# Two mixture-of-experts stages in one long kernel: the token dispatch is split around a turn, and two shared chunks move into the last expert

## The chip, the cores and the metric

The kernel runs on 1 core of one Trainium2 chip. The metric is the device time of one execution in microseconds (us), the median of several runs. The engines are named as in the profile: PE is TensorE's matmul, PEld its weight load, DVE is VectorE, ACT is ScalarE, POOL is GpSimd, SP is SyncE, whose queue issues the weight loads.

## What is computed

The reference is one forward pass over a residual stream `x` of 256 tokens of width 768, with eight layers that alternate graph layers and feed-forward layers:

```
x = x + L0_gnn(layernorm(x));  x = x + L0_ffn(layernorm(x))
x = x + L1_gnn(layernorm(x));  x = x + L1_ffn(layernorm(x))
x = x + L2_gnn(layernorm(x));  x = x + L2_ffn(layernorm(x))
x = x + L3_gnn(layernorm(x));  x = x + L3_ffn(layernorm(x))
```

The change touches two of the eight. Both route each token to its two best of 8 experts and add an expert that all tokens share:

```
L0_ffn: gates = top2(softmax(x @ router)), renormalized
        routed = sum_e gate_e * (silu(x @ Wg_e) * (x @ Wu_e)) @ Wd_e       # 768 -> 768 -> 768
        shared = (silu(x @ Wsg) * (x @ Wsu)) @ Wsd                         # inner width 384
        out    = alpha * shared + (1 - alpha) * routed
L3_ffn: attention, then t = rmsnorm(x)
        routed = the same form, inner width 384;  shared = the same form, inner width 768
        out    = x + routed + shared
```

## The kernel before, in words

Each stage is written as one function for each engine (`L0_ffn_pe`, `L0_ffn_dve` and so on), and each engine works through its functions in order. Nothing is scheduled by a planner: the order on each engine is the order of the code, and engines meet at semaphores (`mark` counts one up when an instruction ends, `at` with `wait_ge` waits for it). Weights stream through a ring of five slots of 2304 KB (`weight_ring`). A load is issued by SP when the unit that held its slot five units before is done with (`unit_free`), and PE waits for it with `loaded`.

Tokens are packed. For each expert 96 places (`NARROW`) are kept for its tokens. `select_dve` (line 995) builds for expert e a one-hot matrix `S` (token by place) with two instructions, and then the same one-hots weighed by the gate, `SA` (the first 64 places) and `SB` (the other 32), with four instructions. One mark, `selected`, stands behind all six. Experts go by pairs: `pair_dispatch_pe` (1048) multiplies the tokens by `S` of both experts of a pair, 24 products of 192 columns in three parts (f = 0,1; 2,3; 4,5), and each part fills a PSUM bank. `pair_xd` (1183) copies a part to the tile `xd`: DVE copies the first and the third, ACT the second. In L3_ffn the copy also multiplies by a norm weight and takes two instructions. The banks are 7, 4, 7 in L0_ffn and 7, 6, 7 in L3_ffn, so the third part waits for the copy of the first.

`weights_turn` (1064) turns `SA` (and for every second pair `SB`) into bank 7, after the third part's copy, and `cb_copy` (1255) has ACT copy the result to `cbA` and `cbB`. `combine_A` and `combine_B` (1077, 1086) use these to add the experts' outputs (`outA`, `outB`) to the accumulators in banks 0 to 3.

One expert on PE (`packed_pe` 1150 in L0_ffn; `both_experts_pe` 1322 in L3_ffn) is this order: the gate and up products from `xd`; `beside_silu_pe` (1095), work put where the silu and the product `h` are being made; the turn of `h` (`packed_hidden_pe` 1128, `both_turn_pe` 1307); `beside_copies_pe` (1104), work put where ACT copies the turned rows to `hT`; the down product from `hT` into banks 7 and 6, which `expert_out_dve` and `expert_out_act` (1226, 1243) copy out. For even experts the work beside is a combine. For odd experts 1, 3 and 5 all of the next pair's dispatch stands beside the silu, and the turn of the weighed one-hots beside the copies, followed by waits for `cbT` and for ACT's `xd` copy. For the last expert (7) nothing stands in either place. After it `combine_last_pe` (1124) waits for the last outputs, and `shared_pe` (1380) runs the shared expert by chunks of 128 inner columns (3 chunks in L0_ffn, 6 in L3_ffn; 12 products of 256 columns each), then its down product. `shared_act` and `shared_dve` (1409, 1414) make the silu and `h` of each chunk.

In the ACT program (`packed_act` 1263, `both_act` 1362) an odd expert has the order: silu, silu, `xd` copy, `hT` copy, `cb_copy`, output copy.

## Time and profile before

| | us |
|---|---|
| median of 3 runs | 1987.83 (1987.59 to 1987.91) |
| the profiled execution | 1986.52 |
| its span in the trace | 1984.5 |
| PE busy | 1845.8 (93% of the span) |
| DVE busy | 704.4 (35%) |
| ACT busy | 439.0 (22%) |
| POOL busy | 299.4 (15%) |

The span is the time from the first to the last instruction on the core; 2.0 us of the profiled execution lie around it. In the trace the routed part of L0_ffn lies from 642.3 to 834.5 us and its shared part ends at 857.96; the routed part of L3_ffn lies from 1809.2 to 1933.2 us and its shared part ends at 1979.9. A row of the timeline gives the start, the duration, the engine, the line of the helper that emitted the instruction, the operation, output and inputs, and the count of merged instructions; in brackets stands how long the engine was idle before it and what it waited for.

### The profile page before, as it was taken

The numbers are of one execution on the slowest core, as the hardware profiler recorded it, in microseconds if no ns is written. First come the engines' busy times: TensorE is split into PE (matmuls) and PEld (weight loads), VectorE is DVE, ScalarE is ACT, GpSimd is POOL, SyncE is SP. The second block draws the span as 40 slices with busy tenths as digits, with TensorE's granted clock in tenths as the row PEclk, the third lists the DMA queues.
The fourth block names the chain that finished last, engine by engine and source line by source line (L and its number), as shares of the span: only waits on it lengthen the run. The fifth ranks groups of instructions, "written<-read, shape, count | busy, mean of one in ns | idle before, by whom it ended". The sixth has DMA issues, their size and how long they took to land.

```text
span 1984.5 us, 25550 instructions
## 1 busy us (share of the span) xinstructions
PE 1845.8 (93%) x11292; PEld 1088.4 (55%) x11292; DVE 704.4 (35%) x1257; ACT 439.0 (22%) x778; POOL 299.4 (15%) x173
## 2 busy tenths in 40 slices
PE   7999999999988999989999998878899999998999
PEld 4664444574435655568765433333466654766557
DVE  5315998019997221144231000001312232234220
ACT  0114554115552111033221000000521010131110
POOL 0003887008883000000000000000000000000000
PEclk9999999999999999986999999999999999998999
DMA  9215001303002677720337999999734235212650
GB/s 365 99 30 185 0 1 37 154 15 153 0 1 98 239 305 305 275 102 17 133 154 286 425 430 428 427 428 429 292 131 167 109 152 231 97 47 106 254 216 17
DMA packets 33792, 364.18 MB, mean 184 GB/s; under 512 B 6797, under 2 KB 10133, under 8 KB 11690
## 3 DMA queue, kind: packets, MB, share of 16 engines
q1 hardware_dynamic: 29568, 358.35, 45.3%
q10 hardware_dynamic: 4106, 4.10, 0.7%
q8 instruction: 93, 1.52, 0.3%
q14 instruction: 25, 0.20, 0.0%
HBM read 356.93 MB, written 0.79 MB: 180 GB/s over the span
## 4 chain that ended last, share of the span: by engine, by line
PE 68%; DVE 11%; DMA 10%; POOL 8%; ACT 2%; issue 1%; DVEq 0%; SPq 0%; ACTq 0%
PE banks L114 65%; POOL gate_work L120 8%; DMA weight_ring<-in_L_ffn_c_fc_dram 7%; DVE gate_work L120 6%; PE banks L117 2%; DVE gate_qiT L134 2%; DMA weight_slot_heads<-in_L_ffn_c_proj_e_dram 1%; DMA weight_ring<-in_L_gnn_W_in_dram 1%; DVE stat L250 1%; DVE xn_tok L125 0%; DMA ident<-in_c_ident_dram 0%; DVE xT L137 0%; ACT gat_E L148 0%; ACT banks L148 0%; ACT r_hT L151 0%
## 5 line engine op out<-in xcount | busy, mean ns | idle before, releaser
L120 POOL TENSOR_TENSOR gate_work<-gate_work 128x1024 f32<-128x1024 f32 x144 | 284.4, 1989 | 319.5 <-DVE gate_work L120 315.7
L114 PE MATMUL banks<-gate_sel,gate_rows 96*128 96x512 bf16 x1152 | 279.0, 380 | 28.4 <-DVE gate_work L120 28.2
L114 PE MATMUL banks<-weight_ring,xT 128*128 128x384 f32 x864 | 292.2, 490 | 2.4 <-DVE rgat_xr L137 1.5
L120 DVE TENSOR_TENSOR gate_work<-banks,gate_qT 128x1024 f32<-128x1024 f32 x192 | 226.2, 1219 | 11.0 <-ACT banks L148 1.4
L148 ACT ACTIVATE banks<-banks 128x1024 f32<-128x1024 f32 x192 | 193.3, 1008 | 132.0 <-PE banks L114 132.0
L114 PEld LDWEIGHTS banks<-weight_ring,xT 128*128 128x128 f32 x864 | 161.8, 191 | 110.1 <-issue 9.4
L114 PEld LDWEIGHTS banks<-gate_sel,gate_rows 96*128 96x128 bf16 x1152 | 104.4, 97 | 181.1 <-DVE gate_work L120 74.8
L120 POOL TENSOR_TENSOR stat<-stat 128x1 f32<-128x1 f32 (+1 forms) x23 | 14.6, 633 | 1174.6 <-DVE stat L124 1037.0
L114 PE MATMUL banks<-xT,weight_ring 128*128 128x256 f32 x792 | 182.2, 382 | 2.4 <-ACT x_tok L151 1.6
L114 PEld LDWEIGHTS banks<-xT,weight_ring 128*128 128x128 f32 x792 | 151.5, 192 | 28.9 <-issue 1.8
L114 PE MATMUL banks<-weight_ring,moe_xdT 128*64 128x384 f32 x744 | 126.1, 489 | 24.3 <-DMA weight_ring<-in_L_ffn_c_fc_dram 23.3
L114 PE MATMUL banks<-weight_ring,r_xd 128*32 128x384 f32 (+1 forms) x2304 | 142.7, 406 | 0.0
L114 PEld LDWEIGHTS banks<-weight_ring,r_xd 128*32 128x32 f32 x2304 | 76.7, 110 | 63.0 <-issue 54.8
L137 DVE COPY y_tok<-banks 128x384 f32<-128x384 f32 x32 | 17.8, 557 | 251.6 <-PE banks L117 251.6
L114 PEld LDWEIGHTS banks<-weight_ring,moe_xdT 128*64 128x64 f32 x744 | 52.2, 137 | 94.2 <-issue 57.9
L114 PE MATMUL banks<-weight_ring,y_tok 128*64 128x384 f32 x528 | 90.0, 490 | 12.2 <-DMA weight_ring<-in_L_ffn_c_proj_e_dram 12.2
L134 DVE TENSOR_REDUCE gate_qiT<-gate_work 128x32 f32<-128x1024 f32 x96 | 90.9, 947 | 15.7 <-POOL gate_work L120 15.7
L114 PE MATMUL banks<-weight_ring,r_hT 128*32 128x192 f32 (+1 forms) x1152 | 73.2, 407 | 6.7 <-ACT r_cbB L151 3.0
L148 ACT ACTIVATE moe_h_tok<-banks 128x384 f32<-128x384 f32 x32 | 15.7, 491 | 270.4 <-PE banks L114 270.4
L114 PEld LDWEIGHTS banks<-weight_ring,y_tok 128*64 128x64 f32 x528 | 35.9, 137 | 59.4 <-issue 41.7
L114 PEld LDWEIGHTS banks<-weight_ring,r_hT 128*32 128x32 f32 x1152 | 37.7, 110 | 41.7 <-issue 33.2
L120 DVE TENSOR_TENSOR r_h<-banks,r_silu 128x256 f32<-128x256 f32 (+2 forms) x32 | 13.3, 416 | 111.0 <-PE banks L114 78.8
(346 smaller groups left out, 1838.9 us busy)
## 6 DMA issues: line engine op xcount, KB each, us to landing
weight_ring<-in_L_ffn_c_fc_dram SPq DMA_DIRECT2D x31, 2304.0 KB, 25.7
weight_ring<-in_L_ffn_c_proj_e_dram SPq DMA_DIRECT2D x22, 2304.0 KB, 28.8
weight_slot_heads<-in_L_ffn_c_proj_e_dram SPq DMA_DIRECT2D x9, 2304.0 KB, 28.3
weight_ring<-in_L_ffn_w_gate_dram SPq DMA_DIRECT2D x8, 2304.0 KB, 9.0
weight_ring<-in_L_ffn_w_up_dram SPq DMA_DIRECT2D x8, 2304.0 KB, 8.7
weight_ring<-in_L_ffn_w_down_dram SPq DMA_DIRECT2D x8, 2304.0 KB, 9.4
weight_ring<-in_L_ffn_w_dram SPq DMA_DIRECT2D x16, 1152.0 KB, 8.1
weight_ring<-in_L_gnn_W_dram SPq DMA_DIRECT2D x7, 2304.0 KB, 14.0
```

What stands on the lines that cost most here:

```text
L114: return self.e.matmul(out, lhsT, rhs, start=start, stop=stop)
L117: return self.e.transpose(out, src, self.ident[0:n, 0:n])
L120: return self.e.tensor_tensor(out, a, b, op)
L134: return self.e.tensor_reduce(out, a, AX.X, op)
L137: return self.e.tensor_copy(out, a)
L148: return self.e.activation(out, a, f, **kw)
L250: t = v.e.bn_stats(half_stats[:, c, h, :], src[:, 2 * c + h, :])
```

## The change

The same arithmetic is done in another order and with other banks. Nothing is removed and nothing is added to what is computed.

- `select_dve` now ends after the two one-hots, and `selected` is marked there. A new `weigh_dve` does the four weighed one-hots and marks `weighed`. For the first pair both selects run before both weighs; for later experts a weigh follows its select.
- The dispatch takes its parts as an argument. For odd experts 1, 3 and 5, `beside_silu_pe` does `weights_turn` and then the first part; `beside_copies_pe` does the second and third. The banks of the parts are 4, 7, 4 in L0_ffn and 6, 7, 4 in L3_ffn. The second part of a later pair waits for `cbT`.
- `weights_turn` waits for `weighed` and no longer for the `xd` copy. It uses bank 5 for the first pair and 7 for the others. PE's wait for `cbT` of the first pair moves from before the first down product to amid the first up products.
- On ACT `cb_copy` now stands before the `hT` copy and the second `xd` copy behind it. On DVE, in L0_ffn, the third `xd` copy moves behind the small `hT` copy.
- In expert 7 the first shared chunk's gate products stand beside the silu and its up products beside the copies. The second chunk stands at the head of `combine_last_pe`. `shared_pe` runs from the third chunk on. Banks of the chunks are 4, 5, 6 in L0_ffn and 6, 5, 4, 7 in turn in L3_ffn, where the narrow part of expert 7's down product goes to bank 4 (`out_bank`) in place of 6.

```diff
         def select_dve(v, B, e):
...
+            if e >= 2:
+                v.wait_ge(*at("pair_sent", (s, e // 2 - 1, 2)))
+                v.wait_ge(*at("weighed", (s, e - 2)))
+            for c in range(TC):
+                t = v.ts(S[:, c, NARROW * z:NARROW * (z + 1)], iota_slot[:, 0:NARROW], slot[:, c, e:e + 1], ALU.is_equal,
+                         mask[:, c, e:e + 1], ALU.mult)
+            t.then_inc(*mark("selected", (s, e)))
+
+        def weigh_dve(v, B, e):
+            s, z, gate, S = B["stage"], e % 2, B["gt"], B["S"]
+            v.wait_ge(*at("selected", (s, e)))
             if e >= 2:
                 v.wait_ge(*at("weights_turned", (s, e // 2 - 1)))
-            for c in range(TC):
-                t = v.ts(S[:, c, NARROW * z:NARROW * (z + 1)], iota_slot[:, 0:NARROW], slot[:, c, e:e + 1], ALU.is_equal,
-                         mask[:, c, e:e + 1], ALU.mult)
-            v.then(t)
             for c in range(TC):
...
-            t.then_inc(*mark("selected", (s, e)))
+            t.then_inc(*mark("weighed", (s, e)))
...
         def sent_bank(B, i):
-            return second_bank(B) if i == 1 else 7
+
+            return (4 if B["hc"] == DC else 6, 7, 4)[i]
...
-            for f in range(DC):
-                if f == 2 and p and B["hc"] == DC:
+            for f in (f for i in part for f in (2 * i, 2 * i + 1)):
+                if f == 0 and p and B["hc"] == DC:
                     pe.wait_ge(*at("routed_silu", (s, 2 * p - 1, 0)))
-                elif f == 4:
+                elif f == 2 and p:
+                    pe.wait_ge(*at("cbT", (s, p)))
+                elif f == 4 and B["hc"] == DC:
                     pe.wait_ge(*at("xd_dve", (s, p, 0)))
+                elif f == 4 and p:
+                    pe.wait_ge(*at("routed_h", (s, 2 * p - 1, 1)))
...
+        def weights_bank(p):
+            return 7 if p else 5
+
         def weights_turn(pe, B, p):
 
             s = B["stage"]
-            pe.wait_ge(*at("xd_dve", (s, p, 2)))
+            pe.wait_ge(*at("weighed", (s, 2 * p + 1)))
+            if p:
+                wait_expert_out(pe, B, 2 * p - 2)
...
         def beside_silu_pe(pe, B, e):
 
             p = e // 2
-            if e % 2:
-                if p + 1 < NEXP // 2:
-                    pair_dispatch_pe(pe, B, p + 1)
+            if e == NEXP - 1:
+                if B["hc"] == DC:
+                    pe.wait_ge(*at("routed_silu", (B["stage"], e, 0)))
+                else:
+                    wait_expert_out(pe, B, e - 1)
+                shared_gate_pe(pe, B["shared"], 0)
+            elif e % 2:
+                weights_turn(pe, B, p + 1)
+                pair_dispatch_pe(pe, B, p + 1, (0,))
             elif p:
                 combine_A(pe, B, p - 1, (0,) if p % 2 else (0, 1))
 
         def beside_copies_pe(pe, B, e):
 
             p, s = e // 2, B["stage"]
-            if e % 2:
-                if p + 1 < NEXP // 2:
-                    weights_turn(pe, B, p + 1)
+            if e == NEXP - 1:
+                shared_up_pe(pe, B["shared"], 0)
+            elif e % 2:
+                pair_dispatch_pe(pe, B, p + 1, (1, 2))
...
-            if e == 0:
-                pe.wait_ge(*at("cbT", (s, 0)))
-            elif e % 2 == 0:
+            if e:
                 wait_expert_out(pe, B, e - 1)
-            elif p + 1 < NEXP // 2:
-                pe.wait_ge(*at("cbT", (s, p + 1)))
+            if e % 2 and e < NEXP - 1:
+                pe.wait_ge(*at("xd_dve", (s, p + 1, 0)))
                 pe.wait_ge(*at("xd_act", (s, p + 1, 1)))
 
+        def out_bank(B, e):
+
+            return 4 if e == NEXP - 1 and B["hc"] < DC else 6
+
         def combine_last_pe(pe, B):
+            shared_gate_pe(pe, B["shared"], 1)
+            shared_up_pe(pe, B["shared"], 1)
             combine_A(pe, B, NEXP // 2 - 1, (0, 1))
             combine_B(pe, B, NEXP // 4 - 1)
...
+        def first_pair_dve(v, B):
+            select_dve(v, B, 0)
+            select_dve(v, B, 1)
+            weigh_dve(v, B, 0)
+            weigh_dve(v, B, 1)
+            pair_xd(v, B, 0, 0, "dve")
+            pair_xd(v, B, 0, 2, "dve")
+
...
         def packed_act(a, B):
...
                 if e % 2 and e + 1 < NEXP:
-                    pair_xd(a, B, e // 2 + 1, 1, "act")
+                    cb_copy(a, B, e // 2 + 1)
                 a.wait_ge(*at("hidden_turned", (s, e)))
                 a.copy(B["hT"][:, 0:512], PS[:, 5, :]).then_inc(*mark("hidden_T_act", (s, e)))
                 if e % 2 and e + 1 < NEXP:
-                    cb_copy(a, B, e // 2 + 1)
+                    pair_xd(a, B, e // 2 + 1, 1, "act")
                 expert_out_act(a, B, e)
...
+        def shared_bank(hc, o):
+            return (4, 5, 6)[o] if hc < DC else (6, 5, 4, 7)[o % 4]
...
+        def shared_pe(pe, shared):
+            key, hc, gate_u, up_u, down_u, h = shared
+            for o in range(2, hc):
+                shared_gate_pe(pe, shared, o)
+                shared_up_pe(pe, shared, o)
```

## Rows read from the trace of the kernel before

**Rows 1.** The page: shares of the chain that ended last, by engine.
```profile
PE 68%; DVE 11%; DMA 10%; POOL 8%; ACT 2%; issue 1%; DVEq 0%; SPq 0%; ACTq 0%
```

**Rows 2.** Chain in order of time, L0_ffn's start: start, duration, what.
```profile
642.39 0.49 DVE r_S L125 x2
...
644.84 0.14 issue
644.98 5.73 PE banks L114 x24
```

**Rows 3.** Timeline of PE, L3_ffn: first dispatch and first turn.
```profile
1811.82 5.85 PE L114 MATMUL banks<-r_S,xn_tok 128*128 128x192 f32 x24 [2.91 <-DVE r_SB L124]
1818.50 0.44 PE L117 MATMUL banks<-ident,r_SA 128*128 128x128 f32 x2 [0.84 <-DVE r_xd L124]
```

**Rows 4.** Timeline of PE, L0_ffn: wait for the third copy, first turn, first expert.
```profile
651.35 0.44 PE L117 MATMUL banks<-ident,r_SA 128*128 128x128 f32 x2 [0.65 <-DVE r_xd L137]
651.72 11.85 PE L114 MATMUL banks<-weight_ring,r_xd 128*32 128x384 f32 x192
```

**Rows 5.** Timeline of PE, L0_ffn, experts 1 and 3 up to the down product.
```profile
683.25 4.17 PE L114 MATMUL banks<-r_S,xn_tok 128*128 128x192 f32 x24
...
688.10 0.40 PE L117 MATMUL banks<-ident,r_SA 128*128 128x128 f32 x2
688.34 0.38 PE L117 MATMUL banks<-ident,r_SB 128*128 128x128 f32 x2
689.49 6.03 PE L114 MATMUL banks<-weight_ring,r_hT 128*32 128x384 f32 x96 [0.77 <-ACT r_cbB L151]
...
734.27 6.03 PE L114 MATMUL banks<-weight_ring,r_hT 128*32 128x384 f32 x96 [0.71 <-ACT r_cbA L151]
```

**Rows 6.** Timeline of PE and ACT, L3_ffn, experts 1 and 3 up to the down product.
```profile
1835.96 4.17 PE L114 MATMUL banks<-r_S,xn_tok 128*128 128x192 f32 x24
...
1838.86 0.73 ACT L148 ACTIVATE r_xd<-banks,small 128x192 f32<-128x192 f32 x2 [2.53 <-PE banks L114]
...
1842.35 3.12 PE L114 MATMUL banks<-weight_ring,r_hT 128*32 128x384 f32 x48 [0.74 <-ACT r_cbB L151]
...
1869.66 3.12 PE L114 MATMUL banks<-weight_ring,r_hT 128*32 128x384 f32 x48 [0.46 <-ACT r_cbA L151]
```

**Rows 7.** Timeline of PE, expert 7 of L0_ffn and after it.
```profile
822.74 6.03 PE L114 MATMUL banks<-weight_ring,r_hT 128*32 128x384 f32 x96 [0.72 <-ACT r_hT L151]
829.29 2.82 PE L114 MATMUL banks<-r_outA,r_cbA 128*128 128x384 f32 x8 [0.52 <-DVE r_outA L137]
...
834.52 15.70 PE L114 MATMUL banks<-xT,weight_ring 128*128 128x256 f32 x72
```

**Rows 8.** Timeline of PE, expert 7 of L3_ffn and after it.
```profile
1922.16 0.33 PE L117 MATMUL banks<-ident,r_h 128*128 128x128 f32 x1 [0.66 <-DVE r_h L120]
...
1923.69 3.12 PE L114 MATMUL banks<-weight_ring,r_hT 128*32 128x384 f32 x48 [0.62 <-ACT r_hT L151]
1927.91 2.85 PE L114 MATMUL banks<-r_outA,r_cbA 128*128 128x384 f32 x8 [1.10 <-DVE r_outA L137]
```

**Rows 9.** Windows: PE, PEld, DVE, ACT, POOL busy, granted clock, DMA share, GB/s.
```profile
647.00:648.00 1.00, 1.00 (x5) 1.00 (x5) 0.09 (x1) 0.00 (x0) 0.00 (x0) 0.50 0.00 0
648.00:649.00 1.00, 1.00 (x7) 1.00 (x7) 0.47 (x1) 0.00 (x0) 0.00 (x0) 0.90 0.00 0
```

**Rows 10.** Timeline of SP's queue: loads of the shared weights, L0_ffn and L3_ffn.
```profile
799.65 0.33 SPq L154 DMA_DIRECT2D weight_ring<-in_L_ffn_ws_gate_dram  x1
...
1909.03 0.33 SPq L154 DMA_DIRECT2D weight_ring<-in_L_ffn_Wsu_dram  x1
```

**Rows 11.** DMA issues from 1840 us on: count, KB each, median us to landing.
```profile
weight_ring<-in_L_ffn_Wsu_dram SPq DMA_DIRECT2D x1, 2304.0 KB, 9.2
```

**Rows 12.** The page: DMA issues over the whole span, the most frequent one.
```profile
weight_ring<-in_L_ffn_c_fc_dram SPq DMA_DIRECT2D x31, 2304.0 KB, 25.7
```

**Rows 13.** The page: the group of L1_ffn's expert products, idle time last.
```profile
L114 PE MATMUL banks<-weight_ring,moe_xdT 128*64 128x384 f32 x744 | 126.1, 489 | 24.3 <-DMA weight_ring<-in_L_ffn_c_fc_dram 23.3
```

More of the change, by code:

```diff
@@ L995, in select_dve @@
         def select_dve(v, B, e):
-            s, z, slot, mask, gate, S = B["stage"], e % 2, B["slot"], B["sc"][1], B["gt"], B["S"]
+            s, z, slot, mask, S = B["stage"], e % 2, B["slot"], B["sc"][1], B["S"]
             if e >= 2:
-                v.wait_ge(*at("weights_turned", (s, e // 2 - 1)))
+                v.wait_ge(*at("pair_sent", (s, e // 2 - 1, 2)))
+                v.wait_ge(*at("weighed", (s, e - 2)))
             for c in range(TC):
@@ L1169, in packed_pe @@
                 pe.wait_ge(*loaded(ukey))
+                if e == 0:
+                    pe.wait_ge(*at("cbT", (s, 0)))
                 wide_part_pe(pe, 5, xd, uw, DC, mark("routed_up", (s, e, 0)))
@@ L1257, in cb_copy @@
             a.wait_ge(*at("weights_turned", (s, p)))
-            t = a.copy(B["cbA"][:, p % 2, :], PS[:, 7, 0:T])
+            t = a.copy(B["cbA"][:, p % 2, :], PS[:, weights_bank(p), 0:T])
             if p % 2:
-                t = a.copy(B["cbB"][:], PS[:, 7, T:2 * T])
+                t = a.copy(B["cbB"][:], PS[:, weights_bank(p), T:2 * T])
             t.then_inc(*mark("cbT", (s, p)))
@@ L1299, in both_pe @@
             t.then_inc(*mark("routed_up", (s, e, 0)))
+            if e == 0:
+                pe.wait_ge(*at("cbT", (s, 0)))
             for k in range(DC):
@@ new lines, in shared_bank, with shared_gate_pe @@
+        def shared_bank(hc, o):
+            return (4, 5, 6)[o] if hc < DC else (6, 5, 4, 7)[o % 4]
+        def shared_gate_pe(pe, shared, o):
+            key, hc, (gkey, g0), (ukey, u0), down_u, h = shared
+            w = w3(unit(gkey, g0, DC * hc * P), DC, hc * P)
+            if o >= 4:
+                pe.wait_ge(*at("shared_h", (key, o - 4)))
+            pe.wait_ge(*loaded(gkey))
+            for k in range(DC):
+                t = pe.mm(PS[:, shared_bank(hc, o), 0:T], w[:, k, o * P:(o + 1) * P], xT[:, k, :], k == 0, k == DC - 1)
+            if o == hc - 1 and gkey != ukey:
+                t.then_inc(*mark("unit_free", gkey))
@@ new lines, in shared_up_pe @@
+        def shared_up_pe(pe, shared, o):
+            key, hc, gate_u, (ukey, u0), down_u, h = shared
+            w = w3(unit(ukey, u0, DC * hc * P), DC, hc * P)
+            pe.wait_ge(*loaded(ukey))
+            for k in range(DC):
+                t = pe.mm(PS[:, shared_bank(hc, o), T:2 * T], w[:, k, o * P:(o + 1) * P], xT[:, k, :], k == 0, k == DC - 1)
+            if o < hc - 1:
+                t.then_inc(*mark("shared_up", (key, o)))
+            else:
+                t.then_inc(*mark("unit_free", ukey))
@@ L1532, in build @@
             shared_t0 = sb("silu", [P, 4, T], F32, st)
-        R0_PARTS = (("L0s", 0), ("L0s", DC * HALF))
+        R0["shared"] = "r0", DC // 2, ("L0s", 0), ("L0s", DC * HALF), "L0sd", shared_h0
         def L0_ffn_sp(q):
@@ L1558, in L0_ffn_pe @@
             packed_pe(pe, R0)
-            shared_pe(pe, "r0", DC // 2, *R0_PARTS, "L0sd", shared_h0)
+            shared_pe(pe, R0["shared"])
             taken_branch(pe, R0, over_pe)
@@ L3045, in build @@
         R3["weight"] = smalls("L3_ffn")[0][0][:, 1, :]
+        R3["shared"] = "r3", DC, ("L3sg", 0), ("L3su", 0), "L3sd", shared_h3
         QKV3 = ["L3q", "L3k", "L3v"]
@@ L3082, in L3_ffn_pe @@
             both_experts_pe(pe, R3)
-            shared_pe(pe, "r3", DC, ("L3sg", 0), ("L3su", 0), "L3sd", shared_h3)
+            shared_pe(pe, R3["shared"])
             taken_branch(pe, R3, over_pe)
```

60 lines of the change are left out of this document (19 added, 41 removed).

## The prediction

> **What bounds the kernel now.** I read the page first: PE is busy for 93% of the span (the table above) and stands for 68% of the chain that ended last [rows 1]. The chain through the two routed parts alternates long stretches of PE with short links of DVE and ACT, so I read the timeline of PE there and took its idle time in brackets, with what ended it. PE's own work does not change, so all that the change can give is that idle time. What bounds each place:
>
> - Before the first pair's dispatch PE waits for six DVE instructions, of which it needs only the one-hots [rows 2, 3].
> - After the dispatch it waits for the third `xd` copy, then turns the weighed one-hots, and only then starts the first expert [rows 4, 3].
> - In experts 1, 3 and 5 the down product waits for ACT, which first copies `hT` and then `cbA` (and `cbB`) [rows 5, 6]. That is three places in each stage, six in all.
> - Expert 7 has nothing to put beside its silu, its copies and its last outputs, and PE stands still at each [rows 7, 8]. Expert 0 has the same gaps and the change leaves them alone.
>
> **The change part by part.** Durations are from the one profiled execution (1986.52 us, span 1984.5). It is 1.3 us under the median of 1987.83. I work out a gain from the trace and take it off the median.
>
> *The first dispatch.* From the first one-hot instruction to the dispatch it takes 644.98 - 642.39 = 2.59 us [rows 2]. Behind the change two selects stand there, 2 x 0.49, and the step to PE, 0.14: 1.12 us. The start moves forward by 1.47 us, to about 643.5. The eight weighing instructions, about 1.3 us, then run beside the dispatch, and the first copy on DVE isn't due until a third of the dispatch is through, about 2.9 us in, so they are hidden; without that cover they would come back in full. What the earlier start is worth depends on the clock. The granted clock is half (1.2 of 2.4 GHz) until 648.2: the window from 647 us shows 0.50 and the one from 648 shows 0.90 [rows 9]. If the rise stays at that moment, the 1.47 us earlier are half-speed time and give 0.73 us; if it moves along with the work, all 1.47. In L3_ffn the dispatch starts at 1811.82 after the same instructions [rows 3], begins at full clock and then runs through one stretch at half. Starting earlier, it has the same stretch in it, and the start gives 1.4 us. I take 0.75 and 1.40.
>
> The Trainium skill says in TensorE: Matmul & The Clock Gate, part 1 (The HAM clock gate), that the monitor which grants the clock is free-running and does not restart with a kernel's work. By that rule the rise stays at 648.2 and the first dispatch gives 0.73 us; by the reading that the clock rises a fixed time after work resumes it would be 1.47. The trace has one first dispatch in each stage and cannot tell the two apart.
>
> *The first turn.* PE waits 0.65 us for the third copy, turns, and starts the expert 0.37 us after the turn began (651.72 - 651.35) [rows 4]. With bank 5 the turn stands in the wait. That gives 0.37 us in L0_ffn and, with the same turn behind a wait of 0.84 us, 0.37 in L3_ffn [rows 3]. The wait for `cbT` is now amid the first up products; ACT's copy takes under 0.4 us while six us of products run, so it costs nothing.
>
> *Experts 1, 3, 5.* PE does the same 24 dispatch products and the same turns. The turn of the weighed one-hots goes first, so ACT's copies of them fall beside the first part (a third of 4.0 us, 1.33) and before `hT`. Behind the turn of `h` stand the second and third parts, 16 products, 2.67 us. The copy of `hT` alone, which in expert 7 costs PE 0.72 us in L0_ffn and 0.62 in L3_ffn [rows 7, 8], is hidden under them. The idle time goes: 0.77 and 0.71 us in L0_ffn [rows 5], 0.74 and 0.46 in L3_ffn [rows 6], and expert 5 is as expert 1. To this comes the drain of the last turn, which an idle PE sees and a busy one doesn't: the two turns of `SB` take 0.38 us, but a busy PE starts the next work after 0.24, as from `SA` at 688.10 to `SB` at 688.34; that is 0.14 at each place; in L3_ffn the turn also waited some 0.15 us for the last `xd` copy. Sum: 2.25 + 3 x 0.14 = 2.67 us in L0_ffn; 1.94 + 3 x 0.29 = 2.81 in L3_ffn. From the idle figures alone it is 4.19 in all, my lower bound; 5.48 is the value I take.
>
> What is late next is ACT's second `xd` copy, now behind `hT`. In L3_ffn, expert 1, PE's up product ends at 1835.96; turn 0.5, first part 1.33, turn of `h` 0.8, second part 1.33 bring the second part's end to about 1839.9, seen by ACT at 1840.2; the copy of 0.73 us [rows 6] ends at 1840.9. PE ends the third part at 1841.25. That is a margin of 0.3 us, the smallest in the change; behind the waiting copy in ACT's queue stands only the output copy, due 3 us later. In L0_ffn the copy is 0.25 us shorter and the margin 0.6. If this cover is gone, each L3_ffn place loses what the copy is late. The first copy, on DVE, has all of the turn of `h` for itself.
>
> *Expert 7 and the shared chunks.* A chunk is 12 of the 72 products that take 15.70 us [rows 7]: 2.62 us, 1.31 for gate or up. Beside the silu PE stood 0.14 us in L0_ffn and 0.66 in L3_ffn, beside the copies 0.72 and 0.62, before the combine 0.52 and 1.10 [rows 7, 8]; each is shorter than what now stands there (1.31, 1.31, 2.62). With about 0.1 us of drain at each of the three: 1.38 + 0.3 = 1.68 and 2.38 + 0.3 = 2.68 us. Those chunks ran without idle time later, so their move costs nothing. It needs the shared weights earlier. L3_ffn's up weights are issued at 1909.03 [rows 10] and land 9.2 us later [rows 11], at 1918.2; the products want them at about 1923.6, and issue and want move forward nearly together. Margin 5 us; L0_ffn has over 10.
>
> *Loads in general.* No load is added. Each waits for its slot, and the slots are freed by the same products, earlier.
>
> *Sum.* L0_ffn: 0.75 + 0.37 + 2.67 + 1.68 = 5.47 us. L3_ffn: 1.40 + 0.37 + 2.81 + 2.68 = 7.26 us. Together 12.7 us. Of the profiled execution that leaves 1973.8, of the median 1975.1.
>
> **The rivals.**
>
> - *The second copy is late (1977.5).* ACT's copy misses its 0.3 us margin in L3_ffn and the turn costs more than reckoned; with the lower bounds for the drains (4.19 in place of 5.48, 0.6 less in expert 7) and 0.2 us of stall in three places the gain is about 10.3. The tight sum above speaks for it, the fact that all other meetings have over 0.5 us against it.
> - *The clock falls differently (1972 or 1978.5).* PE's clock is at half in a dozen stretches outside these parts, and all the work in them moves by 5.5 us. What one stretch costs the rows show: the 24 dispatch products take 5.85 us in L3_ffn's first dispatch, with the clock at half for most of it, and 4.17 in expert 1 [rows 3, 6], 1.7 us more. If the clock keeps to moments of its own, single stretches come or go. Two of them one way or the other are plausible, for both signs, and nothing in the trace settles it. This is what I can't work out.
> - *L0_ffn's part is given back (1980.6).* L1_ffn waits 23.3 us for its weights [rows 13], so DMA bounds it. If its stream of loads doesn't start earlier, 5.5 us vanish and 7.3 remain. Against it: the first of these loads wait for slots that the shared expert of L0_ffn and then L1_ffn's own products free.
> - *The order brings nothing at the copies (1983.5 to 1988, no change to be measured).* That would be so if the down product waited for something other than ACT's copies, its weights say, and only the first dispatch and turn gained (2.9 us). Against it: the idle time is put down to `cbB` and `cbA` [rows 5, 6], and expert 3, which copies `cbA` alone, waits less.
> - *Slower: the shared weights come late (1989.6).* In expert 7 the chunk stands ahead of the turn of `h` in PE's strict order, so a late load holds up the expert itself. Where loads crowd, one took 25.7 us to land [rows 12]. At that, L3_ffn's would land at 1934.7 and be 11 us late, and L0_ffn's, issued at 799.65 [rows 10] and wanted at about 822, some 3.5 us late: 14.5 us lost against 12.7 gained. It decides from a landing time of about 24 us; the measured 9.2 [rows 11] is far from it.
>
> **How the numbers follow.** Forecast 1975.1: 0.62. Late copy: 0.09. Clock, to the fast side 0.09, to the slow side 0.10. Given back: 0.05. Nothing at the copies: 0.03. Slower: 0.02. The forecast's own bounds: the drains and idle figures alone take 1.9 us off, the first dispatch moving with the clock adds 0.7, so 1974.4 to 1977. The range takes in the clock on both sides and the late copy, and with the low bounds of these cases it reaches from 1971.5 to 1979.5. A measurement of this kernel can tell about 0.2% (4 us) from no change. Faster by more than that, under 1983.9: 0.95. Within: 0.03. Slower: 0.02.
>
> **What would show it.** In the changed trace the first dispatch should start at about 643.5, with the one-hots of both experts in one run ahead of it, and the first expert right after the third copy. In experts 1, 3 and 5 the down product should follow the dispatch with no idle time and with no ACT in brackets; a bracket that names ACT's `r_xd` would show the late copy. From the end of the up product to the down product in L0_ffn's expert 1 it should take about 5.3 us where it took 6.2. In expert 7 no idle time over 0.1 us should remain, and no bracket should name a DMA. L0_ffn's shared part should end at about 852.5. From there to the start of L3_ffn's routing the distance should stay at what it was; if it doesn't, the clock or L1_ffn's stream has moved, and the prediction is wrong by that much.

## The result

The changed kernel takes 1969.55 us in the median of four runs (1967.63 to 1972.03), the kernel before 1987.71 beside it: a ratio of 0.9911, with an interval from 0.9894 to 0.9928. It is faster, by 18.2 us where 12.7 were forecast, and the time lies 2 us under the range that was given. The profiled execution is the slowest of the four, 1972.03 us with a span of 1969.9, so the two traces show 14.6 us of difference and not 18.2. Where those 14.6 lie comes first, and then what the other runs add.

The page of the changed kernel, busy time and shares of the chain (rows of before: [rows 1]):

```profile
PE 1843.6 (94%) x11292; PEld 1083.5 (55%) x11292; DVE 704.3 (36%) x1257; ACT 439.1 (22%) x778; POOL 299.1 (15%) x173
PE 67%; DVE 11%; DMA 10%; POOL 8%; ACT 1%; issue 1%; SPq 0%; DVEq 0%; ACTq 0%
```

PE's instructions are the same number. Timeline of PE in the changed kernel, L0_ffn's start and expert 1 (rows of before: [rows 2, 4, 5]); a row gives start, duration, instruction, and in brackets the idle time before it with what ended it:

```profile
642.04 1.21 PE L114 MATMUL banks<-gates_row,selrow 1*128 1x256 f32 x2 [0.57 <-DVE gates_row L137]
644.82 6.13 PE L114 MATMUL banks<-r_S,xn_tok 128*128 128x192 f32 x24 [1.56 <-DVE r_S L125]
650.79 0.38 PE L117 MATMUL banks<-ident,r_SA 128*128 128x128 f32 x2
651.60 11.85 PE L114 MATMUL banks<-weight_ring,r_xd 128*32 128x384 f32 x192 [0.43 <-DVE r_xd L137]
...
682.98 0.44 PE L117 MATMUL banks<-ident,r_SA 128*128 128x128 f32 x2
683.25 0.38 PE L117 MATMUL banks<-ident,r_SB 128*128 128x128 f32 x2
683.47 1.47 PE L114 MATMUL banks<-r_S,xn_tok 128*128 128x192 f32 x8
684.77 0.49 PE L117 MATMUL banks<-ident,r_h 128*128 128x128 f32 x3
685.19 0.33 PE L114 MATMUL banks<-ident,r_h 64*64 64x64 f32 x4
685.46 0.33 PE L117 MATMUL banks<-ident,r_h 128*128 128x128 f32 x1
685.62 2.77 PE L114 MATMUL banks<-r_S,xn_tok 128*128 128x192 f32 x16
688.32 6.03 PE L114 MATMUL banks<-weight_ring,r_hT 128*32 128x384 f32 x96
```

The wait ahead of the first dispatch now ends with a one-hot (`r_S`), where it ended with a weighed one. In expert 1 no bracket is left between the turn of the weighed one-hots and the down product. From the end of the up product to the down product it is 688.32 - 682.98 = 5.34 us; it was 689.49 - 683.25 = 6.24 [rows 5].

The same view in L3_ffn, the first dispatch (rows of before: [rows 3]) and expert 7 with what follows it ([rows 8]):

```profile
1804.38 4.17 PE L114 MATMUL banks<-r_S,xn_tok 128*128 128x192 f32 x24 [1.42 <-DVE r_S L125]
1808.38 0.38 PE L117 MATMUL banks<-ident,r_SA 128*128 128x128 f32 x2
1809.38 6.03 PE L114 MATMUL banks<-weight_ring,r_xd 128*32 128x384 f32 x96 [0.62 <-DVE r_xd L124]
...
1909.17 2.86 PE L114 MATMUL banks<-xT,weight_ring 128*128 128x256 f32 x12
1911.86 0.27 PE L117 MATMUL banks<-ident,r_h 128*128 128x128 f32 x1
1912.06 0.65 PE L114 MATMUL banks<-ident,r_h 64*64 64x64 f32 x28
1912.64 2.86 PE L114 MATMUL banks<-xT,weight_ring 128*128 128x256 f32 x12
1915.43 3.12 PE L114 MATMUL banks<-weight_ring,r_hT 128*32 128x384 f32 x48
1918.48 5.45 PE L114 MATMUL banks<-xT,weight_ring 128*128 128x256 f32 x24
1923.76 2.74 PE L114 MATMUL banks<-r_outA,r_cbA 128*128 128x384 f32 x8
```

Two things are to be seen. The dispatch takes 4.17 us where it took 5.85: it runs at full clock from end to end. And expert 7 has no bracket any more.

Put against each other by the starts of the same instructions, the two traces differ so:

The routing's product of L0_ffn is the one with `gates_row` and `selrow`, that of L3_ffn the one with `r_route` and `before`; the shared down product is the first with `shared_h`.

| stretch, measured on PE | before | after | gain |
|---|---|---|---|
| up to L0_ffn's routing, same code | 641.02 | 642.04 | -1.0 |
| L0_ffn: from there to the shared down product | 209.04 | 203.60 | 5.4 |
| from there to L3_ffn's routing (1807.95; 1802.00), same code | 957.89 | 956.36 | 1.5 |
| L3_ffn: from there to the shared down product | 156.31 | 147.64 | 8.7 |

That is 14.1 us in the two stages that were changed. The rest of the 14.6 lies in stages whose code is the same. The further 3.6 us up to the 18.2 of the medians are in runs without a trace; two traces can't place them.

### The profile page after: what moved, and what is told of

Its sections match the earlier page's. It is cut to its first block, busy times and chain, and to the rows that moved or that the text cites. A ratio compares the mean times of both kernels' runs of the same rounds, so it can differ in the third digit from the quotient of the medians.

```text
span 1969.9 us, 25563 instructions
## 1 busy us (share of the span) xinstructions
PE 1843.6 (94%) x11292; PEld 1083.5 (55%) x11292; DVE 704.3 (36%) x1257; ACT 439.1 (22%) x778; POOL 299.1 (15%) x173
## 4 chain that ended last, share of the span: by engine, by line
PE 67%; DVE 11%; DMA 10%; POOL 8%; ACT 1%; issue 1%; SPq 0%; DVEq 0%; ACTq 0%
PE banks L114 65%; POOL gate_work L120 8%; DMA weight_ring<-in_L_ffn_c_fc_dram 7%; DVE gate_work L120 6%; PE banks L117 2%; DVE gate_qiT L134 2%; DMA weight_slot_heads<-in_L_ffn_c_proj_e_dram 1%; DMA weight_ring<-in_L_gnn_W_in_dram 1%; DVE stat L250 1%; DVE xn_tok L125 0%; SPq L154 0%; DMA ident<-in_c_ident_dram 0%; DVE xT L137 0%; ACT gat_E L148 0%; DVE stat L252 0%
## 5 line engine op out<-in xcount | busy, mean ns | idle before, releaser
L120 POOL TENSOR_TENSOR stat<-stat 128x1 f32<-128x1 f32 (+1 forms) x23 | 14.5, 631 | 1167.3 <-DVE stat L124 1032.2
```

Of the source, the lines that this page charges most:

```text
L120: return self.e.tensor_tensor(out, a, b, op)
```

## The experiments

How much an execution of one kernel varies turned out to matter. Over the comparisons 92 undisturbed runs of the kernel before lie between 1979.7 and 1996.1 us, with a mean of 1987.9 and a standard deviation of 3.3; the three runs shown ahead of the prediction, 0.3 us apart, gave a wrong picture of it. So differences below are between means, against those 92 runs, with 95% intervals worked out from the scatter of both. "Stage" is what one trace shows for L0_ffn or L3_ffn by the marks of the table above.

**The changed kernel again.** No edit.

> The changed kernel once more. From the two traces 5.4 us were gained in L0_ffn and 8.7 in L3_ffn, 1.5 between them, and 1.0 lost ahead of both, where the code is the same. Theory A: what was measured beyond these two stages is the chance of where half-clock stretches fall in an execution; then more runs give 13 to 15.5 us less than before, and the distance from the end of L0_ffn's shared part to L3_ffn's routing differs from the 948.5 us of the first trace by up to some 3 us. Theory B: the change makes the stages between faster in itself; then the gain stays at 17 to 19 us and that distance at 948 to 949 us.

> The changed kernel a third time, for the mean. The stages L0_ffn and L3_ffn are 14.1 us shorter in both traces so far, but over the runs the mean is 18.7 us (give or take 1.9) under that of before. Theory A, chance of the clock elsewhere: with more runs the difference comes down towards 14 to 16. Theory B, what lies between the two stages becomes faster on the mean: it stays at 17 to 20.

> The changed kernel beside the two above, on the same chip: 1969.3 as before by both theories.

| | span | up to L0_ffn | L0_ffn | between | L3_ffn |
|---|---|---|---|---|---|
| before | 1984.5 | 641.02 | 209.04 | 957.89 | 156.31 |
| after | 1969.9 | 642.04 | 203.60 | 956.36 | 147.64 |
| again | 1967.6 | 642.84 | 203.60 | 953.24 | 147.64 |
| again2 | 1967.5 | 642.99 | 203.62 | 952.99 | 147.64 |
| again3 | 1969.3 | 642.65 | 203.60 | 953.45 | 149.32 |

With the first four, 21 runs have a mean of 1969.3: 18.6 us less than before, give or take 1.1. The ratios of the three comparisons are 0.9906 (0.9891 to 0.9921), 0.9908 (0.9889 to 0.9927) and 0.9900 (0.9882 to 0.9918). L0_ffn is the same to 0.02 us in each trace; L3_ffn is 147.64 in three and 149.32 in one. Theory A, that all beyond the two stages was chance, expected the mean to come down to 14 to 16 and has fallen. The runs of before came from three chips, with means of 1988.1, 1987.0 and 1988.5 us; against the runs on its own chip in the same comparison each repeat is 19.4, 17.9 and 19.2 us faster. What remains beyond the two stages is 4 to 5 us.

**Each stage alone.** All of the change in one stage, the behaviour of before in the other. The edit, shortened to its main lines, for L0_ffn alone (for L3_ffn alone the two names are swapped). Such kernels, here and below, are the changed kernel with parts of it switched off:

```diff
 # as in the changed kernel for B["stage"] == "r0"
 # for B["stage"] == "r3" back to:
-            select_dve(v, B, 0); select_dve(v, B, 1); weigh_dve(v, B, 0); weigh_dve(v, B, 1)
+            select_dve(v, B, 0); weigh_dve(v, B, 0); select_dve(v, B, 1); weigh_dve(v, B, 1)
-                weights_turn(pe, B, p + 1)
-                pair_dispatch_pe(pe, B, p + 1, (0,))
+                pair_dispatch_pe(pe, B, p + 1, (0, 1, 2))
...
-            for o in range(2, hc):
+            for o in range(0, hc):
```

> All of the change in L0_ffn, none in L3_ffn. Both theories: L0_ffn's stage 5.4 us shorter in the trace. Theory A: 5.4 us less in all, give or take 1.5. Theory B: 8 to 9 us less, since what the stages between gain hangs on L0_ffn ending earlier. L3_ffn's first dispatch: 5.85 us (half clock) if the longer wait ahead of it lowers the clock, either 4.2 or 5.9 if that is chance.

> The change in L0_ffn alone, a second time. Its stage is 5.4 us shorter. The changed kernel is 4 to 5 us faster on the mean than its two stages account for. If that comes from the stages between, because L0_ffn ends earlier, it must show here in full: 9.5 to 10 us under before. If it comes from L3_ffn or from both together, 5.4 us.

> All of the change in L3_ffn, none in L0_ffn. From my sum 7.3 us less; from the first trace 8.7, of which 1.7 is the first dispatch at full clock (4.17 us for 24 products in place of 5.85). If the shorter wait ahead of the dispatch (1.4 us in place of 2.9) keeps the clock up, this trace shows 4.2 us again and the gain is 8.7; if it was chance, the dispatch can show 5.9 and the mean gain lies near 7.3 to 8.

> The change in L3_ffn alone, a second time. Nothing ahead of L3_ffn is touched, so the stages between can't gain: 8.3 us under before (8.7 with the first dispatch at full clock, 7.0 where it falls to half, which it did in 2 of 10 traces). If the difference is 12 us or more, the extra belongs to L3_ffn.

L0_ffn alone: stage 203.44 and 203.57 in the two traces, 5.5 us shorter; 14 runs, 7.4 us less than before, give or take 1.6 (ratios 0.9960, 0.9946 to 0.9975, and 0.9966, 0.9953 to 0.9978). L3_ffn alone: stage 147.64 in both traces, 8.7 us shorter; 10 runs, 7.6 us less, give or take 1.5 (0.9954, 0.9941 to 0.9967, and 0.9965, 0.9952 to 0.9978). So the part in L3_ffn gives what its stage shows, within the interval. The part in L0_ffn gives 2.0 us more than its stage, give or take 1.6, and not the 4 that were expected if the extra hung on L0_ffn's earlier end alone. The two halves add to 15.0, give or take 2.2, against 18.6 together. The extra isn't in either half in full. The second run of L0_ffn alone, 7.0 us (give or take 2.2), lies between its two expectations, 9.5 to 10 and 5.4; that of L3_ffn alone, 7.1 (give or take 1.2), is near the 8.3 that were expected and far from 12.

**One kind of edit in both stages.** Three kernels: the starts alone, experts 1, 3 and 5 alone, the shared chunks alone.

```diff
 # starts: against before
-            select_dve(v, B, 0)          # with the weighing inside
-            select_dve(v, B, 1)
+            select_dve(v, B, 0); select_dve(v, B, 1); weigh_dve(v, B, 0); weigh_dve(v, B, 1)
 # and the first turn in bank 5, waiting for "weighed" in place of "xd_dve"
 # odd: against the changed kernel
+            if p == 0:
+                pe.wait_ge(*at("weighed", (s, 1)))      # ahead of the first dispatch
+                pe.wait_ge(*at("xd_dve", (s, 0, 2)))    # ahead of the first turn
 # and shared chunks 0 and 1 back behind the last combine
 # last: against before
+                shared_gate_pe(pe, B["shared"], 0)      # beside expert 7's silu
+                shared_up_pe(pe, B["shared"], 0)        # beside its copies
 # and chunk 1 ahead of the last combine
```

> In both stages only the start is changed: both selects ahead of the weighing, and the first turn in bank 5 without the wait for the third copy. From my sum 0.75 + 0.37 + 1.40 + 0.37 = 2.9 us less. If the shorter wait keeps the clock up in L3_ffn, 4.6 us. If the starts bring nothing, 0.

> In both stages only experts 1, 3 and 5 are changed: the turn of the weighed one-hots first, the dispatch split around the turn of the rows, ACT's copies in the new order. The first pair keeps its old order and waits. By my sum 5.5 us less (2.67 + 2.81), lower bound 4.2; by the first trace of the changed kernel 0.9 us at each of the three places in L0_ffn and 1.0 to 1.1 in L3_ffn. If ACT's second copy were late, a PE wait for r_xd ahead of the down product in L3_ffn would show, and under 5 us.

> In both stages only the two shared chunks are moved into and behind expert 7. By my sum 1.7 + 2.7 = 4.4 us less; lower bound 3.8 from the idle figures alone. If the shared weights came late a PE wait for a DMA would show in expert 7.

| | L3_ffn in the trace | gain there | mean of the runs against before | ratio |
|---|---|---|---|---|
| before | 156.31 | | | |
| starts | 152.95 | 3.4 | -4.7, give or take 2.2 (11 runs) | 0.9973 (0.9959 to 0.9986) |
| odd | 153.58 | 2.7 | -4.4, give or take 2.4 (12 runs) | 0.9984 (0.9968 to 1.0000) |
| last | 154.20 | 2.1 | -4.4, give or take 1.7 (12 runs) | 0.9984 (0.9971 to 0.9997) |

I compare in L3_ffn, since the first dispatch in L0_ffn differs in its clock from trace to trace (its 24 instructions took between 5.7 and 7.0 us in these). The three gains add to 8.2 of the 8.7 us, and each edit gives a part of it. The interval of the second reaches no change in the ratio. The starts give 3.4 us where 1.77 were forecast, and that is the clock. PE in the kernel with the starts alone:

```profile
1812.83 4.17 PE L114 MATMUL banks<-r_S,xn_tok 128*128 128x192 f32 x24 [1.42 <-DVE r_S L125]
1816.84 0.38 PE L117 MATMUL banks<-ident,r_SA 128*128 128x128 f32 x2
```

**Is it the wait that sets the clock of the dispatch?** The kernel before (the changed kernel with all its parts switched off), with products that nobody reads in the wait:

```diff
+            idle_products_pe(pe, 3)      # L0_ffn; 6 in L3_ffn
             pair_dispatch_pe(pe, B, 0)
```

> The kernel before, with products whose result nobody reads put on PE in the wait ahead of the first dispatch: three in L0_ffn, six in L3_ffn, which at full clock fill that wait of 2.9 us. Nothing else is changed and the dispatch starts as late as before. If PE's idling ahead of the dispatch is what sets the clock in it, L3_ffn's 24 products take 4.2 us in place of 5.9 and the whole takes up to 1.7 us less, in L0_ffn up to 1 us less. If the clock there is chance, no systematic change; if the dispatch starts later by the products, up to 1 us more.

PE in this kernel, L3_ffn:

```profile
1808.34 2.84 PE L114 MATMUL banks<-before,ident 128*128 128x256 f32 x12
1811.48 4.14 PE L114 MATMUL banks<-r_S,xn_tok 128*128 128x192 f32 x24 [0.31 <-DVE r_SB L124]
```

The dispatch is at full clock, though it starts as late as before: 3.95 us behind the routing's product, where it was 3.87. L3_ffn is 154.87, 1.4 us shorter; L0_ffn is 208.97, the same. The runs are 4.2 us under before, give or take 1.8 (0.9979, 0.9965 to 0.9994). That is more than the two stages show in the trace; the rest comes back under what stays open. Over all traces of this study, the first dispatch of L3_ffn:

| wait ahead of it | traces | 4.2 us (full clock) | 5.8 to 5.9 us (half for most of it) |
|---|---|---|---|
| 2.9 to 3.0 us | 7 | 0 | 7 |
| 1.4 us | 11 | 9 | 2 |
| filled with products | 2 | 2 | 0 |

One of the two exceptions is the trace of the third repeat of the changed kernel. First its PE, then the windows over the dispatch in that trace and in the second repeat's. Behind the five busy times of a window stands the granted clock, 0.72 and 1.00, then DMA share and GB/s:

```profile
1802.08 5.85 PE L114 MATMUL banks<-r_S,xn_tok 128*128 128x192 f32 x24 [1.42 <-DVE r_S L125]
1807.76 0.38 PE L117 MATMUL banks<-ident,r_SA 128*128 128x128 f32 x2
```

```profile
1802.00:1808.00 6.00, 5.92 (x26) 5.81 (x26) 2.04 (x12) 0.73 (x2) 0.00 (x0) 0.72 0.00 0
```

```profile
1802.00:1808.00 6.00, 5.38 (x42) 4.55 (x46) 3.69 (x18) 2.31 (x4) 0.00 (x0) 1.00 0.01 3
```

So the shorter wait makes the fall rare, and doesn't exclude it: the same code with the same wait can show both.

**What is left at the starts.** The first expert waits 0.43 and 0.62 us for the third copy. Its first rows of products need only the first copy:

```diff
 # against the changed kernel
-            return (4 if B["hc"] == DC else 6, 7, 4)[i]
+            return 6 if p == 0 and i == 2 else (4 if B["hc"] == DC else 6, 7, 4)[i]
...
             for k in range(n):
+                if e == 0 and k % 2 == 0:
+                    pe.wait_ge(*at(("xd_dve", "xd_act", "xd_dve")[k // 2], (B["stage"], 0, k // 2)))
```

> The changed kernel, and beyond it the first expert starts its first products before the third copy of xd is done: its first six rows of products wait for each copy when they need it, and the third part of the first dispatch goes to bank 6. The wait for the third copy (0.4 us in L0_ffn, 0.6 in L3_ffn) and the drain of the turn go: 1.0 to 1.3 us less than the changed kernel. If the copy were not what PE waits for there, nothing.

> The version that starts the first expert before the third copy is done, a second time. In its trace L0_ffn is 0.5 us and L3_ffn 0.7 us shorter than in the changed kernel; so 1.2 us less, 1968.1, if nothing else moves, and up to 1 us either way on top of it if L0_ffn's end being 0.5 us earlier changes what follows.

PE in the first of these two traces, L3_ffn:

```profile
1807.61 4.17 PE L114 MATMUL banks<-r_S,xn_tok 128*128 128x192 f32 x24 [1.42 <-DVE r_S L125]
1811.61 0.38 PE L117 MATMUL banks<-ident,r_SA 128*128 128x128 f32 x2
1811.93 6.03 PE L114 MATMUL banks<-weight_ring,r_xd 128*32 128x384 f32 x96
```

The bracket is gone. L0_ffn is 203.11 and 203.00 and L3_ffn 146.95 in both: 0.5 and 0.7 us under the changed kernel, as expected. The 12 runs have a mean of 1968.8, 0.5 us under the changed kernel's, give or take 1.7. In the time this can't be told from nothing; the trace shows it.

With one product in L0_ffn's wait and three in L3_ffn's on top:

```diff
+            idle_products_pe(pe, 1)      # L0_ffn; 3 in L3_ffn
```

> The version that starts the first expert before the third copy is done, and in addition products that nobody reads in the waits ahead of the first dispatch: one in L0_ffn, three in L3_ffn. L3_ffn's dispatch ran at full clock in every trace with a wait of 1.4 us, so there the products bring nothing and may cost up to 0.3 us. In L0_ffn the clock is at half and a product of about 0.9 us fits in the wait of 1.6; if more activity brings the clock back sooner, up to 0.7 us less, else nothing. Against the changed kernel 1.0 to 1.9 us less.

L0_ffn 203.08, L3_ffn 146.95: nothing in either stage. In L0_ffn the product runs at half clock and the dispatch behind it takes 6.46 us, no less than without it. The mean of 6 runs, 1967.6, isn't apart from the 1968.8 of the version without the products.

**Does what follows L0_ffn depend on when L0_ffn ends?** Theory A: the stages behind it are rigid, and a delay costs its own length. Theory B: their mean time depends on where L0_ffn's end falls against the moments at which the clock can change, in a pattern that repeats, so that some delays cost nothing and others more than they last. The edit is tiny dependent DVE instructions behind L0_ffn's last product, 7 and 17 of them in the kernel before, 2 and 9 in the changed kernel:

```diff
             shared_dve(v, "r0", DC // 2, shared_h0, shared_t0, alphas[:, 0, :])
+            v.wait_ge(*at("unit_free", "L0sd"))
+            for _ in range(7):
+                v.then(v.ts(pad[:], desc[:], 1.0, ALU.mult))
```

> The kernel before with seven tiny dependent DVE instructions behind L0_ffn's last product, about 1.4 us in which nothing else can start. All that follows is put 1.4 us later, and nothing is removed. Theory A: 1.4 us more than before. [...]

> [...] Both theories: 3 to 4 us more than before. It is the control of the run with 1.4 us.

> The changed kernel with a wait of 1.9 to 2.0 us behind L0_ffn's last product (two tiny DVE instructions of 0.2 us and the 1.5 us of issue time that any instruction put there brought in the two traces with delays), so that all that follows starts 3.4 us earlier than in the kernel before, and not 5.4. Nothing else is changed. Theory A (stages behind it are rigid, the rest is chance): 2 us over the changed kernel, 1971.3. [...]

> [...] Both theories: 3.4 us over the changed kernel, 1972.7. By theory B it is faster than the kernel with 2 us of wait although it waits longer; by theory A it is 1.4 us slower than that.

DVE in the kernel with 17, behind L0_ffn:

```profile
860.15 3.45 DVE L124 TENSOR_SCALAR pad<-desc 128x8 f32<-128x8 f32 x17 [6.44 <-PE banks L114]
865.13 1.03 DVE L250 BATCH_NORM_STATS2 stat<-banks 128x6 f32<-128x384 f32 x2 [1.53 <-issue]
```

The delay is larger than I had planned in the first two: 1.53 us of issue time comes on top of the instructions, so they are 1.4 + 1.5 = 2.9 and 3.45 + 1.5 = 5.0 us. In the changed kernel, where I reckoned with it, they are 0.4 + 1.5 = 1.9 and 1.8 + 1.5 = 3.3.

| kernel | delay | expected by A; by B | mean against the kernel without it |
|---|---|---|---|
| before, 7 | 2.9 | +1.4; -1.5 to -3 | +4.0, give or take 1.9 (12 runs) |
| before, 17 | 5.0 | +3 to +4 by both | +0.8, give or take 1.8 (12 runs) |
| changed, 2 | 1.9 | +2; +6.3 | +2.6, give or take 2.5 (6 runs) |
| changed, 9 | 3.3 | +3.4 by both | +0.4, give or take 2.2 (6 runs) |

Against before the ratios of the first two are 1.0022 (1.0007 to 1.0037) and 1.0009 (0.9995 to 1.0024), those of the last two 0.9914 (0.9895 to 0.9934) and 0.9905 (0.9886 to 0.9924). Against the runs of before on their own chip alone the first two are +4.9 and +1.7, give or take 2.3.

If all that follows were rigid (theory A), the second and the fourth would be 5.0 and 3.3; both are under that by more than their interval. So a delay can cost much less than it lasts, and the stages behind are not rigid in the mean. But theory B in the form I gave it falls too: it wanted +6.3 for the third and +3.4 for the fourth. The first two were expected for shorter delays than they had, so they count for the table and not for either theory's numbers.

## Why the prediction was right, and where it wasn't

The measured time lies 2 us below the range. Two steps carry it there. One term was sized too small: L3_ffn's first dispatch and turn gave 3.54 us where 1.77 were forecast. The other was put at nothing: the sum holds only the two changed stages and takes all other stages to keep their time, while 4 to 5 us of the mean gain lie there. With the first term right the sum would be 14.5 us and the forecast 1973.3, still inside the range; it is the second that leads out of it. The steps, with what the first pair of traces shows:

| step | forecast | measured |
|---|---|---|
| L0_ffn, first dispatch and turn | 1.12 | 1.14 |
| L3_ffn, first dispatch and turn | 1.77 | 3.54 |
| L0_ffn, experts 1, 3, 5 | 2.67 | 0.90 + 0.84 + 0.90 = 2.64 |
| L3_ffn, experts 1, 3, 5 | 2.81 | 1.01 + 0.75 + 1.01 = 2.77 |
| L0_ffn, expert 7 and behind it | 1.68 | 1.51 |
| L3_ffn, expert 7 and behind it | 2.68 | 2.35 |
| not foreseen: expert 0 of L0_ffn, wait for `hT` 0.61 for 0.77 | 0 | 0.16 |
| sum of the stages | 12.7 | 14.1 |

*What bounds.* Right. PE's idle time was what there was to gain, and where it was named it went.

*The first dispatch in L0_ffn.* Right in size for this pair of traces. The wait in front of it fell from 3.05 to 1.56 us and the 24 instructions took 6.13 in place of 5.72 us, since more of them ran at half clock; the start came 1.2 us earlier against the product ahead of it (2.78 us behind it in place of 3.96), and with the turn's 0.37 taken off the 1.14 it was worth 0.77. The granted clock is half from 641.4 to 648.2 us in the trace before and from 642.0 to 648.9 in the trace after: the same length, though the dispatch in it began 1.2 us earlier, so the rise did not move along with the work. The page TensorE: Matmul & The Clock Gate of the Trainium skill (part 1) says that the clock's monitor keeps its own time, and this pair of traces agrees: 0.77 is near the value of a rise that stands still, 0.73, and not 1.47. Over all traces the early start is worth more. From the routing's product to the end of the dispatch it takes 9.7 us in five of the seven traces with the long wait and 11.3 in the other two, in which the clock is half for longer, but 8.7 to 8.9 in all eleven with the short one; that is some 0.5 us more in the mean, if two in seven is the true share.

*The first dispatch in L3_ffn.* **The step that failed** is "Starting earlier, it has the same stretch in it". I carried the half-clock stretch over as if it belonged to the dispatch. It belonged to the wait: with 2.9 us of it the dispatch ran at half in seven traces of seven, with 1.4 us in two of eleven, with the wait filled in none of two. The term should have been 1.49 for the start (the dispatch stands 2.38 us behind the routing's product, where it was 3.87) and 1.68 (5.85 - 4.17) for the clock; with 0.37 for the turn that is the 3.54. The price of the stretch stood in the prediction, under the rivals, but was given to other places. The same page and part give the half clock as the level of an idle engine and the full clock as that of a busy one, and the table of the waits goes the same way; that spoke for more gain here and I did not weigh it.

*Experts 1, 3, 5.* Right to 0.04 us in each stage, and the drain of the turn, which the idle figures alone leave out, is in it (4.19 by the idle figures against 5.41 measured). The tight place held. ACT and PE in L3_ffn's expert 1 of the changed kernel:

```profile
1829.05 2.87 PE L114 MATMUL banks<-r_S,xn_tok 128*128 128x192 f32 x16
1829.19 0.40 ACT L151 COPY r_hT<-banks 128x288 f32<-128x288 f32 x1 [1.38 <-PE banks L114]
1830.66 0.73 ACT L148 ACTIVATE r_xd<-banks,small 128x192 f32<-128x192 f32 x2 [1.06 <-PE banks L114]
1831.85 0.83 PE L114 MATMUL banks<-weight_ring,r_hT 128*32 128x384 f32 x5
```

ACT's copy ends at 1831.39 and PE wants it at 1831.85: a margin of 0.46 us where 0.3 was worked out. The rival of the late copy is refuted.

*Expert 7.* The mechanism is right and the size 0.17 and 0.33 us too high: the drain that I added at three places is a guess that the rows did not carry. One number was misread. A chunk is 24 of the 72 rows' instructions and not 12, since each product of four-byte numbers stands in the trace as two (the 24 instructions of a dispatch are 12 products of the code for the same reason); gate or up covers 2.6 us and not 1.3. It changed nothing, as even 1.3 was cover enough. The weights were there in time: no bracket names a DMA. SP issued L3_ffn's up weights at 1896.76, they took 9.6 us to land, and the first product on them started at 1912.64. (The 25.7 us that the last rival takes for one load are the median of 31.)

```profile
1896.76 0.33 SPq L154 DMA_DIRECT2D weight_ring<-in_L_ffn_Wsu_dram  x1
```

```profile
weight_ring<-in_L_ffn_Wsu_dram SPq DMA_DIRECT2D x1, 2304.0 KB, 9.6
```

*What lies between the stages.* This is the term that was put at nothing, and the rival "the clock falls differently" is the one that came, in part. The same code took 953.0 to 957.9 us between the two stages in the five traces of the first table. Most of the difference is in L1_gnn, right behind L0_ffn. Windows from the end of L0_ffn's shared product to the first product of L1_ffn with weights from the ring, in the kernel before, the changed kernel and its second repeat (granted clock 0.70, 0.71, 0.75):

```profile
857.96:936.89 78.93, 70.23 (x307) 59.45 (x307) 42.89 (x103) 31.27 (x73) 2.90 (x7) 0.70 0.11 40
```

```profile
853.54:930.69 77.15, 68.26 (x308) 56.68 (x307) 42.98 (x103) 31.27 (x73) 2.91 (x7) 0.71 0.12 40
```

```profile
854.51:928.36 73.85, 64.95 (x307) 54.24 (x307) 42.94 (x103) 31.27 (x73) 2.92 (x7) 0.75 0.12 41
```

DVE and ACT are busy for the same time in all three; PE has the same instructions and is busy for 5.3 us less in the last. That is the clock alone. It is more than chance of a single trace: in six traces (before, L3_ffn alone twice, starts, odd, last) L0_ffn has none or only a part of the change, and this stretch takes 77.1 to 80.2 us, 79.1 in the mean; in the nine that have all of it and no delay it takes 73.9 to 77.7, 76.2 in the mean. That is 2.9 us less, give or take 1.4. The stretch from there to L3_ffn's routing has a mean of 870.5 and 870.6 us in the same two groups, give or take 1.6. So of what the changed kernel gains outside its two stages the traces show the larger part in L1_gnn, and none in the stages between L1_gnn and L3_ffn.

Over the runs the time follows the clock: a line through all runs, with a level of its own for each kernel, gives 1.55 us for each 0.001 of mean granted clock (0.1 either way), and the mean granted clock of the changed kernel is 0.9793 over 21 runs against 0.9765 over 92. By that line some 4.3 us of the 18.6 are clock, and the rest is 14.3, give or take 0.8. L3_ffn's first dispatch (1.68 us in 9 traces of 11) is some 1.4 us of the clock's part.

*Given back, nothing at the copies, slower:* none of the three came. DMA's share of the chain is 10% as before.

**What stays open.** The changed kernel is 18.6 us faster (give or take 1.1), its stages account for 13.8 (5.4 + 8.7, less 0.3 for the two in eleven dispatches at half clock), or 14.3 with the 0.5 of L0_ffn's first dispatch from above. The other 4 to 5 us are in stages with the same code. That they are less time at half clock is shown in L1_gnn's traces (2.9 us); of the clock's 4.3 us by the line, 2.4 to 2.9 are left for these stages, so up to 2 us are not placed. Three explanations were tried. Pure chance is refuted by 21 against 92 runs. A dependence on where L0_ffn ends that repeats as theory B had it is refuted by the changed kernel with 1.9 us of delay. That the extra hangs on one half of the change is not borne out: 2.0 (give or take 1.6) come with L0_ffn's half, none with L3_ffn's (1.1 less than its stage, give or take 1.5), and 3.6 (give or take 2.5) more only with both. That the stages behind are not rigid is shown, by the delays of 5.0 and 3.3 us that cost 0.8 and 0.4.

One kernel speaks against any explanation by L0_ffn's earlier end alone: the kernel before with unread products in its two waits. L0_ffn ends no earlier in it than before, its stages give 1.4 us, and it is 4.2 us faster (give or take 1.8) at the same mean granted clock as the changed kernel, 0.9793; its trace has L1_gnn at 72.8 us. What it shares with the changed kernel is less idle time of PE at the starts of the two stages. But the kernel with the starts alone shares that too, and its mean clock is 0.9764. Why the stages behind come out on the fast side is not shown.

## What to carry to other kernels

An idle time of an engine is worth more than its length where it decides the clock of what follows: a wait of 2.9 us cost its own time and another 1.7 us in the 24 instructions behind it. Work that doesn't need to be anywhere (a turn, a part of a dispatch, a chunk of an independent product) pays when it is put into waits: idle time plus a drain read from rows gave the gain to 0.04 us a stage at experts 1, 3 and 5, while a drain that was guessed missed by 0.2 and 0.3 us at expert 7. Three runs that agree to 0.3 us don't tell how far runs scatter; before a gain of half a per cent is read, take enough of them to see the scatter, and compare stages in the trace: over four traces of the changed kernel L0_ffn was the same to 0.02 us, and L3_ffn too but for one dispatch at half clock. A sum over the changed stages alone leaves out what the others do at another clock, here 4 to 5 us.

## What the runs showed of the hardware

- The first dispatch in L3_ffn took 4.1 to 4.2 or 5.8 to 5.9 us in 20 traces and nothing between, by the clock it was granted. With a wait of 2.9 to 3.0 us ahead of it, it was the slow one in seven traces of seven, with 1.4 us in two of eleven. Products that nobody reads in the wait kept the clock up (4.14 us).
- In L0_ffn one such product, put in a wait when the clock was already at half, did not bring it back sooner (6.46 us for the dispatch behind it).
- One kernel's executions differ by up to 16 us (1979.7 to 1996.1), in step with the mean granted clock, 1.55 us for each 0.001.
- L1_gnn, with the same code, took 79.1 us in the mean of six traces and 76.2 in the mean of nine in which L0_ffn ahead of it was 5.4 to 6 us shorter.
- Seven dependent DVE instructions of 0.2 us, put behind L0_ffn, cost 1.53 us of issue time more than their own 1.4 us, and the same with two, nine and seventeen.
- A delay of 5.0 us in the chain made the kernel 0.8 us slower (give or take 1.8), and one of 2.9 us in the same place 4.0 us (give or take 1.9).
